# A replicated row in float32 and a carry copy taken out of the scan's signal, in a layer of scan attention and a gated expert network

## The chip, the cores and the metric

The kernel runs on all 8 cores of one Trainium2 chip. Each core takes one of the 8 sequences (2048 tokens of 1024 features); nothing passes between cores. The metric is the device time of the slowest core, in microseconds (us). Engines are named as the profile names them: PE is TensorE's matmul unit, PEld its weight load, DVE VectorE, ACT ScalarE, POOL GpSimd, SP SyncE.

## The reference

```
x = x + attn(layernorm(x));   x = x + ffn(layernorm(x))

attn(x):  h = rmsnorm(x) * gamma
          q, kv, a = split(h @ w_qkva.T)          # 3 x 1024
          y[t] = sigmoid(a[t]) * y[t-1] + kv[t]   # a scan over the 2048 tokens
          return q * y
ffn(x):   gate = softmax(x @ Wg + bg)             # 8 experts
          h = relu(x @ W1[e] + b1[e])             # 1024 -> 128, each expert
          return sum over e of gate[e] * (h @ W2[e] + b2[e])
```

## The kernel before

Everything is held transposed: features on the 128 partitions (8 blocks of 128, `KC = 8`), tokens along the free axis. The 2048 tokens are worked in 4 chunks of `TC = 512`. The whole program is written out by hand, engine by engine: each step is emitted with its engine, and counting semaphores (`s_mm` for PE, `s_dve`, `s_act`, `s_gp`) carry the waits. A semaphore counts the instructions of its engine, so "wait for the scan of block j" means "wait until DVE's count has reached the number that was recorded at that point" (`rec`, `rec_i`). What stands in an engine's queue is done in that order.

One chunk c goes through these steps.

- **Statistics 1** (`emitS1`, `emitSq`, `emitS2`): PE sums x and x squared over the features by a matmul with a column of 1/1024 (L288, L331). `emit_rows` (L218 to L235, DVE) makes one row of means and one of inverse variances, 512 long, on a single partition; ACT takes the square root of the latter (L242). DVE's reciprocal of one row is L235.
- **Replication 1** (`emitRep1`): two matmuls with a contraction of one row copy the two rows to all 128 partitions of PSUM (L347: 1/sigma, L349: mean); ACT takes both to SBUF in one activation (L357, `rm_bf`). DVE then subtracts and multiplies (L370, L384, in chunk 0 L873, L876).
- **emitB**: for each block j eight matmuls for kv (L415), eight for a (L434), two blocks later eight for q (L483). ACT takes the sigmoid (L446), DVE runs the scan (L457) and copies its last column to `carry` (L461), which the next chunk's scan starts from. kv of block j waits for the count recorded as `scan[j-2]`. DVE multiplies by q (L494), POOL adds x (L506).
- **emitC, emitRep2, emitLn2**: ACT casts the result (L521) and squares it (L543), PE sums (L533, L551), `emit_rows` and L242 again, then **replication 2** (L567: 1/sigma, L569: mean) into `ps_rep`. DVE copies both to SBUF for POOL (L577, L578) and normalizes blocks 0 to 4 (L589, L592); POOL does blocks 5 to 7 (L601, L604).
- **Gate and experts**: scores (L627), exp (L635), sum (L645), reciprocal (L656). The gate's reciprocal row is replicated to 8 partitions by a float32 matmul (L668, weights `ones_f`), read by DVE at L678. `emitE1`: eight matmuls for each expert (L724), relu on ACT (L784), the gate replicated (L742, L774), their product on DVE (L755, L805).
- **emitY2grp, emitOuts**: the second expert matmul (L826, L829) and the last addition (L843). For chunk c-1 these stand between the steps of chunk c.

The load of the next chunk's `xbf` is issued by POOL after its last addition of L506, and PE's statistics 1 of chunk c+1 stand in its queue ahead of replication 2 of chunk c. Replication 1 of chunk c+1 stands inside `emitE1` of chunk c, after the matmuls of expert 4. The weights' folds by gamma are L199 (DVE, chunk 0 only).

Of the kernel before, what the change touches and what calls it, by code (L numbers as in the profile page):

```python
# [27 lines left out]
def build_program(T=2048, TC=512):  # L28
# [23 lines left out]
    with stack:  # L52
# [24 lines left out]
        asig = sb("asig", [128, 2, TC], F32)  # L77
        h1g = sb("h1g", [128, E, TC], BF16)
        carry = sb("carry", [128, KC], F32)
        rows = sb("rows", [1, 5 * TC], F32)  # L80
        plscr = sb("plscr", [1, 1], F32)
        rows_bf = sb("rows_bf", [1, 2 * TC], BF16)
        exg = sb("exg", [8, TC], BF16)
        g_bf = sb("g_bf", [8, TC], BF16)

# [2 lines left out]

        def row(i):
            return rows[0:1, i * TC:(i + 1) * TC]  # L90
        R_M, R_T0, R_S2, R_INV, R_GI = 0, 1, 2, 3, 4

        def rowbf(i):
            return rows_bf[0:1, i * TC:(i + 1) * TC]
# [120 lines left out]
        def emit_rows(K, key, eps_add, key_m=None):  # L215
            def _rows(vector):
                vector.wait_ge(s_mm.h, K[key_m or key])
                s_dve.inc(vector.tensor_copy(row(R_M), ps_q[0:1, 0, :]))  # L218
                rec(K, key + "_rdm", s_dve)
                vector.wait_ge(s_dve.h, s_dve.n)  # L220
                s_dve.inc(vector.tensor_copy(rowbf(0), row(R_M)))
                s_dve.inc(vector.tensor_mul(row(R_T0), row(R_M), row(R_M)))
                vector.wait_ge(s_dve.h, s_dve.n)
                vector.wait_ge(s_mm.h, K[key])
                s_dve.inc(vector.scalar_tensor_tensor(row(R_S2), row(R_T0), -1.0,
                                                      ps_q[0:1, 1, :], ALU.mult,
                                                      ALU.add))
                rec(K, key + "_rd", s_dve)
                vector.wait_ge(s_dve.h, s_dve.n)
                if eps_add is None:  # L230
                    s_dve.inc(vector.tensor_scalar_max(row(R_S2), row(R_S2), 1e-33))
                else:
                    s_dve.inc(vector.tensor_scalar_add(row(R_S2), row(R_S2), eps_add))
                vector.wait_ge(s_dve.h, s_dve.n)
                ii = vector.reciprocal(row(R_INV), row(R_S2))  # L235
                s_dve.inc(ii)
            on("vector", _rows)
            rec(K, key + "_row1", s_dve)

            def _r(scalar):  # L240
                scalar.wait_ge(s_dve.h, K[key + "_row1"])
                ii = scalar.activation(rowbf(1), row(R_INV), AF.Sqrt)  # L242
                s_act.inc(ii)
            on("scalar", _r)
            rec(K, key + "_actr", s_act)

# [95 lines left out]
        def emitRep1(c):  # L342
            K = ck[c]

            def _rep(tensor):
                tensor.wait_ge(s_act.h, K["mm_s2_actr"])
                tensor.matmul(ps_q[:, 0, :], ones_bf[0:1, :], rowbf(1),  # L347
                              start=True, stop=True)
                ii = tensor.matmul(ps_q[:, 1, :], ones_bf[0:1, :], rowbf(0),  # L349
                                   start=True, stop=True)  # L350
                s_mm.inc(ii)
# [39 lines left out]
        def emitB(c):  # L391
# [9 lines left out]
            for j in range(KC):  # L401
# [52 lines left out]
                def _scan(vector, j=j):  # L454
# [2 lines left out]
                    s_dve.inc(vector.tensor_tensor_scan(y_sb[:, j, :], asig[:, j % 2, :],  # L457
                                                        ps_kv[:, j % 2, :], init,
                                                        ALU.mult, ALU.add))
                    vector.wait_ge(s_dve.h, s_dve.n)  # L460
                    ii = vector.tensor_copy(carry[:, j:j + 1], y_sb[:, j, TC - 1:TC])  # L461
                    s_dve.inc(ii)
                on("vector", _scan)
                rec_i(K["scan"], j, s_dve)

                if j >= 2:
                    emit_q(c, j - 2)
# [92 lines left out]
        def emitRep2(c):  # L560
            K = ck[c]

            def _rep(tensor):
                tensor.wait_ge(s_act.h, K["mm_s2b_actr"])
                if c > 0:
                    tensor.wait_ge(s_dve.h, ck[c - 1]["h1g"][E - 1])
                tensor.matmul(ps_rep[:, 0, :], ones_bf[0:1, :], rowbf(1),  # L567
                              start=True, stop=True)
                ii = tensor.matmul(ps_rep[:, 1, :], ones_bf[0:1, :], rowbf(0),  # L569
                                   start=True, stop=True)  # L570
# [436 lines left out]
```

## Time and profile before

| what | value |
|---|---|
| median of 2 runs | 511.88 us (511.72 to 512.03) |
| the profiled execution, its own time | 511.4 us |
| its span on core 0, the slowest | 509.9 us |
| spans of the 8 cores | 497.2 to 509.9 us |
| busy PE / DVE / ACT / POOL | 397.4 / 236.7 / 113.6 / 102.0 us |
| mean granted TensorE clock, core 0 | 0.894 of full speed |

The profile records one execution. A span runs from a core's first to its last instruction; 1.5 us of the execution's time lie outside it. "Busy" adds up the instructions' durations, so it tells how much an engine has to do and not whether the end waits for it. A matmul's duration holds its way through the array; the distance between the starts of two matmuls in a row tells what one costs in a stream.

### The profile page before, as it was taken

What the parts mean: (1) busy time and instruction counts of PE and PEld (TensorE: products, weight loads), DVE (VectorE), ACT (ScalarE), POOL (GpSimd) and SP (SyncE); (2) the same over time, 40 slices, a digit from 0 to 9 for tenths busy, and PEclk for the clock granted to TensorE, in tenths of its full rate; (3) what the DMA queues carried; (4) which work ended last, traced back from release to release, by engine and by line L of the source; (5) the groups of instructions that cost most, each with busy time, mean ns of one, the idle gap of its engine ahead of it and who ended that gap; (6) DMA issues with size and microseconds to landing.
All of it is one profiled execution on the core that took longest, in us unless ns stands there. A gap on an engine that the chain in (4) does not pass through costs nothing.

```text
span 509.9 us, 4752 instructions; the slowest of 8 cores (497.2 to 509.9 us)
## 1 busy us (share of the span) xinstructions
PE 397.4 (78%) x1532; PEld 146.3 (29%) x1532; DVE 236.7 (46%) x356; ACT 113.6 (22%) x179; POOL 102.0 (20%) x76
## 2 busy tenths in 40 slices
PE   1425399834778999759879999759989998888893
PEld 0101144300222444213323444213323443233331
DVE  0364433443466434337475344427475343783221
ACT  1220001350124112610222102610233115402200
POOL 6000012402800021308300023109100113050000
PEclk9955789986597999978988999978999999999997
DMA  7999995091000000560400000740400000004004
GB/s 137 214 171 156 160 171 86 0 227 21 0 0 2 0 1 1 144 104 1 165 1 1 1 0 2 170 77 1 165 0 2 1 0 1 1 0 165 2 0 165
DMA packets 18231, 32.06 MB, mean 63 GB/s; under 512 B 656, under 2 KB 4752, under 8 KB 18208
## 3 DMA queue, kind: packets, MB, share of 16 engines
q0 software_dynamic: 9584, 14.98, 19.5%
q1 hardware_dynamic: 8624, 16.79, 10.1%
q8 instruction: 13, 0.21, 0.2%
q14 instruction: 10, 0.08, 0.1%
HBM read 38.35 MB, written 8.39 MB: 92 GB/s over the span
## 4 chain that ended last, share of the span: by engine, by line
PE 60%; DMA 17%; DVE 11%; issue 3%; ACT 2%; another core or an unknown queue 2%; POOL 1%; DVEq 0%; ACTq 0%; POOLq 0%
PE ps_kv L415 11%; PE ps_a L434 10%; PE ps_q L483 10%; DMA xbf<-xT 10%; PE ps_kv L724 8%; DMA wq_bf<-wqT 8%; PE ps_a L829 6%; PE ps_kv L829 3%; DVE rows L235 3%; PE ps_a L724 3%; PE ps_q L288 2%; PE ps_a L627 1%; PE ps_rep L774 1%; DVE wq_bf L199 1%
## 5 line engine op out<-in xcount | busy, mean ns | idle before, releaser
L506 POOL TENSOR_TENSOR x_sb<-x_sb,y_sb 128x512 f32<-128x512 f32 x32 | 40.5, 1266 | 268.3 <-DVE y_sb L494 268.2
L415 PE MATMUL ps_kv<-hbf,wq_bf 128*128 128x512 bf16 x256 | 67.4, 393 | 18.0 <-DVE carry L461 8.3
L434 PE MATMUL ps_a<-hbf,wq_bf 128*128 128x512 bf16 x256 | 62.7, 389 | 4.9 <-DVE wq_bf L199 4.9
L457 DVE TENSOR_TENSOR_SCAN y_sb<-asig,carry,ps_kv 128x512 f32<-128x512 f32 x24 | 30.7, 1280 | 62.5 <-ACT asig L446 62.5
L483 PE MATMUL ps_q<-hbf,wq_bf 128*128 128x512 bf16 x256 | 59.2, 379 | 0.0
L446 ACT ACTIVATE asig<-ps_a 128x512 f32<-128x512 f32 x32 | 19.1, 597 | 158.8 <-PE ps_a L434 158.8
L724 PE MATMUL ps_kv<-hbf,w_bf 128*128 128x512 bf16 x192 | 48.6, 407 | 0.0
L288 PE MATMUL ps_q<-xbf,statc 128*1 128x512 bf16 x32 | 14.4, 624 | 36.5 <-DMA xbf<-xT 36.5
L415 PEld LDWEIGHTS ps_kv<-hbf,wq_bf 128*128 128x128 bf16 x256 | 25.3, 99 | 55.8 <-issue 30.4
L434 PEld LDWEIGHTS ps_a<-hbf,wq_bf 128*128 128x128 bf16 x256 | 25.3, 100 | 36.9 <-issue 8.7
L829 PE MATMUL ps_a<-h1g,w_bf 128*128 128x512 bf16 x128 | 34.0, 414 | 0.0
L483 PEld LDWEIGHTS ps_q<-hbf,wq_bf 128*128 128x128 bf16 x256 | 25.0, 98 | 30.2 <-issue 0.6
L829 PE MATMUL ps_kv<-h1g,w_bf 128*128 128x512 bf16 x128 | 31.9, 394 | 0.0
L601 POOL TENSOR_TENSOR y_sb<-x_sb,asig 128x512 f32<-128x512 f32 x12 | 15.2, 1267 | 79.6 <-DVE asig L578 79.6
L805 DVE TENSOR_TENSOR h1g<-y_sb,ps_rep 128x512 bf16<-128x512 f32 x24 | 16.2, 685 | 23.8 <-ACT y_sb L784 16.3
L235 DVE RECIPROCAL rows<-rows 1x512 f32<-1x512 f32 x8 | 26.7, 3341 | 0.8
L724 PEld LDWEIGHTS ps_kv<-hbf,w_bf 128*128 128x128 bf16 x192 | 18.7, 103 | 26.2 <-issue 9.0
L784 ACT ACTIVATE y_sb<-ps_kv,b1s 128x512 f32<-128x512 f32 x24 | 16.0, 677 | 43.2 <-PE ps_kv L724 43.2
L494 DVE TENSOR_TENSOR y_sb<-ps_q,y_sb 128x512 f32<-128x512 f32 x32 | 22.1, 691 | 7.4 <-PE ps_q L483 6.5
L218 DVE COPY rows<-ps_q 1x512 f32<-1x512 f32 x8 | 5.4, 676 | 34.5 <-PE ps_q L288 18.0
L315 POOL TENSOR_TENSOR tbf<-xbf 128x4096 bf16<-128x4096 bf16 x3 | 21.0, 7012 | 0.0
L211 ACT ACT_TABLE_LOAD x16 | 20.5, 1283 | 1.5 <-ACT y_sb L784 0.4
(82 smaller groups left out, 382.7 us busy)
## 6 DMA issues: line engine op xcount, KB each, us to landing
x_sb<-xT SPq DMA_DIRECT2D x4, 2048.0 KB, 13.2
outT<-x_sb SPq DMA_DIRECT2D x4, 2048.0 KB, 6.9
wq_bf<-wqT POOLq DMA_DIRECT2D x3, 2048.0 KB, 39.3
xbf<-xT POOLq DMA_DIRECT2D x3, 1024.0 KB, 16.3
w_bf<-w1p POOLq DMA_DIRECT2D x1, 2048.0 KB, 63.8
w_bf<-w2p POOLq DMA_DIRECT2D x1, 2048.0 KB, 75.6
xbf<-xT POOLq DMA_DIRECT2D x2, 512.0 KB, 11.9
wg_bf<-wgp POOLq DMA_DIRECT2D x1, 256.0 KB, 75.6
```

The lines of the kernel that those rows point to most:

```text
L211: ii = scalar.activation(plscr[:], plscr[:], func)
L235: ii = vector.reciprocal(row(R_INV), row(R_S2))
L288: ii = tensor.matmul(ps_q[0:1, 0, :], statc[:], xbf[:, k, :], start=(k == 0), stop=(k == KC - 1))
L315: ii = gpsimd.tensor_tensor(xsq[:], xbf[:], xbf[:], ALU.mult)
L415: ii = tensor.matmul(ps_kv[:, j % 2, :], wq_bf[:, k, (8 + j) * 128:(9 + j) * 128], hbf[:, k, :], start=(k == 0), stop=(k == KC - 1))
L434: ii = tensor.matmul(ps_a[:, j % 2, :], wq_bf[:, k, (16 + j) * 128:(17 + j) * 128], hbf[:, k, :], start=(k == 0), stop=(k == KC - 1))
L457: s_dve.inc(vector.tensor_tensor_scan(y_sb[:, j, :], asig[:, j % 2, :], ps_kv[:, j % 2, :], init, ALU.mult, ALU.add))
L483: ii = tensor.matmul(ps_q[:, j % 2, :], wq_bf[:, k, j * 128:(j + 1) * 128], hbf[:, k, :], start=(k == 0), stop=(k == KC - 1))
L494: ii = vector.tensor_tensor(y_sb[:, j, :], ps_q[:, j % 2, :], y_sb[:, j, :], ALU.mult)
L506: ii = gpsimd.tensor_tensor(x2buf(c)[:, j, :], x_sb[:, j, :], y_sb[:, j, :], ALU.add)
L724: ii = tensor.matmul(pb[:, BM[e] % 2, :], w1_bf[:, k, e * 128:(e + 1) * 128], hbf[:, k, :], start=(k == 0), stop=(k == KC - 1))
L829: ii = tensor.matmul(pb[:, d % 2, :], w2_bf[:, e, d * 128:(d + 1) * 128], h1g[:, e, :], start=False, stop=(e == E - 1))
```

## The change

Two things change. First, the row of 1/sigma is written by ACT in float32 (a new row `R_R` of `rows`, which grows from 5 to 6 rows; `rows_bf` shrinks to one) and not in bfloat16, and both matmuls that replicate it (L347, and L567 which becomes L569) take float32 weights (`ones_f`) and this float32 row. The row of means stays bfloat16. There are 8 such matmuls: replication 1 and replication 2 of 4 chunks. Second, the count that others wait for as `scan[j]` is recorded right behind the scan and no longer behind the carry copy, and in the last chunk, which no other follows, the copy and DVE's wait for the scan ahead of it are left out (8 copies of 32).

```diff
--- before.py
+++ after.py
@@ -77,9 +77,9 @@
         asig = sb("asig", [128, 2, TC], F32)
         h1g = sb("h1g", [128, E, TC], BF16)
         carry = sb("carry", [128, KC], F32)
-        rows = sb("rows", [1, 5 * TC], F32)
+        rows = sb("rows", [1, 6 * TC], F32)
         plscr = sb("plscr", [1, 1], F32)
-        rows_bf = sb("rows_bf", [1, 2 * TC], BF16)
+        rows_bf = sb("rows_bf", [1, TC], BF16)
         exg = sb("exg", [8, TC], BF16)
         g_bf = sb("g_bf", [8, TC], BF16)
 
@@ -88,7 +88,7 @@
 
         def row(i):
             return rows[0:1, i * TC:(i + 1) * TC]
-        R_M, R_T0, R_S2, R_INV, R_GI = 0, 1, 2, 3, 4
+        R_M, R_R, R_T0, R_S2, R_INV, R_GI = 0, 1, 2, 3, 4, 5
 
         def rowbf(i):
             return rows_bf[0:1, i * TC:(i + 1) * TC]
@@ -239,7 +239,7 @@
 
             def _r(scalar):
                 scalar.wait_ge(s_dve.h, K[key + "_row1"])
-                ii = scalar.activation(rowbf(1), row(R_INV), AF.Sqrt)
+                ii = scalar.activation(row(R_R), row(R_INV), AF.Sqrt)
                 s_act.inc(ii)
             on("scalar", _r)
             rec(K, key + "_actr", s_act)
@@ -344,7 +344,7 @@
 
             def _rep(tensor):
                 tensor.wait_ge(s_act.h, K["mm_s2_actr"])
-                tensor.matmul(ps_q[:, 0, :], ones_bf[0:1, :], rowbf(1),
+                tensor.matmul(ps_q[:, 0, :], ones_f[0:1, :], row(R_R),
                               start=True, stop=True)
                 ii = tensor.matmul(ps_q[:, 1, :], ones_bf[0:1, :], rowbf(0),
                                    start=True, stop=True)
@@ -457,11 +457,13 @@
                     s_dve.inc(vector.tensor_tensor_scan(y_sb[:, j, :], asig[:, j % 2, :],
                                                         ps_kv[:, j % 2, :], init,
                                                         ALU.mult, ALU.add))
-                    vector.wait_ge(s_dve.h, s_dve.n)
-                    ii = vector.tensor_copy(carry[:, j:j + 1], y_sb[:, j, TC - 1:TC])
-                    s_dve.inc(ii)
+                    rec_i(K["scan"], j, s_dve)
+                    if c + 1 < NCH:
+                        vector.wait_ge(s_dve.h, s_dve.n)
+                        ii = vector.tensor_copy(carry[:, j:j + 1],
+                                                y_sb[:, j, TC - 1:TC])
+                        s_dve.inc(ii)
                 on("vector", _scan)
-                rec_i(K["scan"], j, s_dve)
 
                 if j >= 2:
                     emit_q(c, j - 2)
@@ -564,7 +566,7 @@
                 tensor.wait_ge(s_act.h, K["mm_s2b_actr"])
                 if c > 0:
                     tensor.wait_ge(s_dve.h, ck[c - 1]["h1g"][E - 1])
-                tensor.matmul(ps_rep[:, 0, :], ones_bf[0:1, :], rowbf(1),
+                tensor.matmul(ps_rep[:, 0, :], ones_f[0:1, :], row(R_R),
                               start=True, stop=True)
                 ii = tensor.matmul(ps_rep[:, 1, :], ones_bf[0:1, :], rowbf(0),
                                    start=True, stop=True)
```

PE's queue in chunk 0, from the gate of expert 3 over replication 1 of chunk 1 to the matmuls of expert 5 (`g_bf` is the gate, `sel_bf` the selection matrix, `w_bf` the experts' weights). Before:

```order
L774 MATMUL ps_rep<-g_bf,sel_bf 128x512
L724 MATMUL ps_a<-hbf,w_bf 128x512 x8
L347 MATMUL ps_q<-rows_bf,ones_bf 128x512
L349 MATMUL ps_q<-rows_bf,ones_bf 128x512
L774 MATMUL ps_rep<-g_bf,sel_bf 128x512
L724 MATMUL ps_a<-hbf,w_bf 128x512 x8
```

and now:

```order
L776 MATMUL ps_rep<-g_bf,sel_bf 128x512
L726 MATMUL ps_a<-hbf,w_bf 128x512 x8
L347 MATMUL ps_q<-rows,ones_f 128x512
L349 MATMUL ps_q<-rows_bf,ones_bf 128x512
L776 MATMUL ps_rep<-g_bf,sel_bf 128x512
L726 MATMUL ps_a<-hbf,w_bf 128x512 x8
```

Nothing has moved; L347 alone reads `rows` and `ones_f`, both float32, in the place of `rows_bf` and `ones_bf`.

DVE's queue at the end of `emitB` in the last chunk: the last two scans (the order calls them SCALAR_TENSOR_TENSOR, the profile TENSOR_TENSOR_SCAN), the products with q and the start of the statistics. Before:

```order
L457 SCALAR_TENSOR_TENSOR y_sb<-asig,carry,ps_kv 128x512
L461 COPY carry<-y_sb 128x1
L494 TENSOR_TENSOR y_sb<-ps_q,y_sb 128x512
L457 SCALAR_TENSOR_TENSOR y_sb<-asig,carry,ps_kv 128x512
L461 COPY carry<-y_sb 128x1
L494 TENSOR_TENSOR y_sb<-ps_q,y_sb 128x512 x3
L218 COPY rows<-ps_q 1x512
```

and now:

```order
L457 SCALAR_TENSOR_TENSOR y_sb<-asig,carry,ps_kv 128x512
L496 TENSOR_TENSOR y_sb<-ps_q,y_sb 128x512
L457 SCALAR_TENSOR_TENSOR y_sb<-asig,carry,ps_kv 128x512
L496 TENSOR_TENSOR y_sb<-ps_q,y_sb 128x512 x3
L218 COPY rows<-ps_q 1x512
```

The copies are gone, so each product with q stands right behind a scan. In the chunks 0 to 2 they stand as before.

## Rows read from the trace of the kernel before

A row of the timeline gives the start (us from the span's start), the duration in us (of all, from the first start to the last end, where xN follows), the engine, the line, the operation, output<-input, and in brackets the idle time of the engine before it and what ended that.

**Rows 1.** The page's chain of work that ended last, shares of the span by engine.
```profile
PE 60%; DMA 17%; DVE 11%; issue 3%; ACT 2%; another core or an unknown queue 2%; POOL 1%; DVEq 0%; ACTq 0%; POOLq 0%
```

**Rows 2.** Timeline, chunk 0: first scan, its carry copy, and kv of block 2.
```profile
60.40 1.21 DVE L457 TENSOR_TENSOR_SCAN y_sb<-asig,ps_kv 128x512 f32<-128x512 f32 x1
61.72 0.15 DVE L461 COPY carry<-y_sb 128x1 f32<-128x1 f32 x1
...
62.02 3.57 PE L415 MATMUL ps_kv<-hbf,wq_bf 128*128 128x512 bf16 x8 [8.31 <-DVE carry L461]
```

**Rows 3.** Timeline, chunk 3: replication 2, then the float32 replication of the gate.
```profile
442.98 0.37 PE L567 MATMUL ps_rep<-rows_bf,ones_bf 1*128 1x512 bf16 x1 [1.43 <-ACT rows_bf L242]
...
443.67 0.69 DVE L577 COPY asig<-ps_rep 128x512 f32<-128x512 f32 x1 [0.53 <-PE ps_rep L569]
...
452.76 1.89 PE L627 MATMUL ps_a<-hbf,wg_bf 128*128 128x512 bf16 x8 [0.69 <-DVE x_sb L843]
...
465.35 1.02 PE L668 MATMUL ps_a<-rows,ones_f 1*8 1x512 f32 x2
...
466.54 0.68 DVE L678 TENSOR_TENSOR g_bf<-exg,ps_a 8x512 bf16<-8x512 bf16 x1 [5.51 <-PE ps_a L668]
```

**Rows 4.** Timeline, chunk 1: replication 2 and what follows until the scores.
```profile
228.69 0.60 PE L567 MATMUL ps_rep<-rows_bf,ones_bf 1*128 1x512 bf16 x1
...
229.82 0.69 DVE L577 COPY asig<-ps_rep 128x512 f32<-128x512 f32 x1 [8.50 <-PE ps_rep L569]
...
230.08 3.59 PE L829 MATMUL ps_a<-h1g,w_bf 128*128 128x512 bf16 x8
...
237.96 1.27 POOL L604 TENSOR_TENSOR hbf<-y_sb,asig 128x512 bf16<-128x512 f32 x1
...
240.19 1.89 PE L627 MATMUL ps_a<-hbf,wg_bf 128*128 128x512 bf16 x8
```

**Rows 5.** Timeline, chunk 0: replication 2 and the experts' first three groups.
```profile
121.19 0.56 PE L567 MATMUL ps_rep<-rows_bf,ones_bf 1*128 1x512 bf16 x1
...
122.07 0.69 DVE L577 COPY asig<-ps_rep 128x512 f32<-128x512 f32 x1 [9.15 <-PE ps_rep L569]
...
133.74 7.76 PE L724 MATMUL ps_kv<-hbf,w_bf 128*128 128x512 bf16 x24
```

**Rows 6.** Timeline, chunk 0: end of replication 1 for chunk 1, next matmul.
```profile
152.91 0.63 PE L349 MATMUL ps_q<-rows_bf,ones_bf 1*128 1x512 bf16 x1
...
154.32 0.58 PE L774 MATMUL ps_rep<-g_bf,sel_bf 8*128 8x512 bf16 x1 [0.78 <-DVE h1g L805]
```

**Rows 7.** Timeline, chunk 1: the same for chunk 2, and expert 5.
```profile
263.95 0.37 PE L347 MATMUL ps_q<-rows_bf,ones_bf 1*128 1x512 bf16 x1 [2.45 <-ACT rows_bf L242]
...
265.38 0.58 PE L774 MATMUL ps_rep<-g_bf,sel_bf 8*128 8x512 bf16 x1 [0.84 <-DVE h1g L805]
...
265.90 3.59 PE L724 MATMUL ps_a<-hbf,w_bf 128*128 128x512 bf16 x8
```

**Rows 8.** Timeline, chunk 2: expert 5 behind replication 1 for chunk 3.
```profile
378.65 1.90 PE L724 MATMUL ps_a<-hbf,w_bf 128*128 128x512 bf16 x8
```

**Rows 9.** Timeline, start: replication 1 of chunk 0 evacuated, then the fold.
```profile
29.75 1.00 ACT L357 ACTIVATE rm_bf<-ps_q 128x1024 bf16<-128x1024 f32 x1
...
31.08 3.26 DVE L199 TENSOR_SCALAR wq_bf<-wq_bf,gam 128x1024 bf16<-128x1024 bf16 x8 [3.53 <-DMA wq_bf<-wqT]
```

**Rows 10.** Groups by line and form: xcount, then busy us, mean ns, idle before.
```profile
L446 ACT ACTIVATE asig<-ps_a 128x512 f32<-128x512 f32 x32 | 19.1, 597 | 158.8 <-PE ps_a L434 158.8
...
L242 ACT ACTIVATE rows_bf<-rows 1x512 bf16<-1x512 f32 x8 | 5.0, 628 | 59.2 <-DVE rows L235 59.2
```

**Rows 11.** Timeline, last chunk: the product behind the last carry copy.
```profile
425.38 0.69 DVE L494 TENSOR_TENSOR y_sb<-ps_q,y_sb 128x512 f32<-128x512 f32 x1
```

**Rows 12.** Windows, PE: stretch, length, busy (matmuls), granted clock, DMA share, GB/s.
```profile
229.00:232.00 3.00, 3.00 (x8) 0.50 0.00 0
...
265.00:268.00 3.00, 2.62 (x6) 0.50 0.00 0
```

## The prediction

> **What bounds the kernel now.** I read the chain of waits first, then the waits in total, then the timeline around the eight replications. The chain lies on PE for 60% of the span, 17% on DMA, 11% on DVE [rows 1]. PE is not busy all the time, but nearly all that it waits for waits in turn for PE: the load of the next chunk is issued only after the last product of q, and the statistics rows are made from PE's sums. So a delay of PE at most places moves the end by as much, and what must be asked at each of the eight replications is whether PE or DVE stood waiting for something else there. The carry copies are 0.15 us each and DVE is busy for 236.7 of 509.9 us, so they matter only where somebody waits for the signal behind them.
>
> **One float32 replication.** The trace has this form once in each chunk, on the gate's row. One such matmul is recorded in two parts that take 1.02 us together, and DVE starts 1.19 us after its start (466.54 - 465.35) [rows 3]. A bfloat16 matmul at the same clock takes 0.37 us, and DVE starts 0.69 us after the first of the two of replication 2 (443.67 - 442.98) [rows 3]; one of them costs (1.90 - 0.37)/7 = 0.22 us in a stream [rows 8], so a single one would release DVE after 0.47 us. The float32 form thus costs 1.02 - 0.37 = 0.65 us more by durations and 1.19 - 0.47 = 0.72 us by release; I take 0.70. It is 0.65/0.22 = 3 further passes. At half clock a pass is (3.59 - 0.60)/7 = 0.43 us [rows 4], so the extra is 3 x 0.43 = 1.28 us there.
>
> The row of the trace loads 8 columns of weights and the new matmuls load 128; a load of bfloat16 weights of 128 columns shows no cost of its own: the distance of 0.22 us above holds one for each matmul. I take 0 and keep +0.2 us for each of the four on the path as the bound (one more pass is 0.22 us), 0.8 in all. The Trainium skill ("TensorE: Matmul & The Clock Gate", section on weight-path perf modes and on LDWEIGHTS) says that the fast weight load isn't used for float32 weights and that a plain load takes the columns divided by 1.2 GHz, 107 ns for 128. No row here shows a float32 load of that width. If two such loads were needed and none were hidden, the estimate by that page is some 0.2 us for each matmul, and the sum below would be 0.8 us higher.
>
> **Replication 2, four times.** In chunk 3 the clock is full. DVE waits for the second matmul (0.53 us, at 443.67) and then works without a pause until the scores, where PE stands 0.69 us waiting for DVE (452.76) [rows 3]. The whole delay goes through: +0.70.
> In chunk 1 (chunk 2 reads the same) the clock is at 0.50 [rows 12]: DVE starts 1.13 us after the first matmul (229.82 - 228.69) and PE goes on at once with L829, eight matmuls in 3.59 us [rows 4]. The extra is 1.28 us. Does DVE's delay show? POOL's last block is ready at 237.96 + 1.27 = 239.23, and its matmul is the last of eight that start at 240.19 [rows 4], about 2.5 us later; both move. So PE alone decides. The clock comes back within L829 in any case; where this moment stays, 1.28 us of matmuls at half speed are pushed out and done later in 0.64 us, and the net cost is 1.28 - 0.64 = +0.64. Where the clock comes back as much later, it is +1.28. I take 0.64 each, 1.3 for both, bounds 1.3 to 2.6.
> In chunk 0 the clock is between the levels: 0.56 us for the first matmul, DVE starts 0.88 us after it (122.07 - 121.19) [rows 5]. Here DVE's normalization paces PE until the scores, and PE idles between; the delay of 0.65 to 1.28 us goes through to 133.74. From there the experts' 24 matmuls take 7.76 us [rows 5], against about 24 x 0.22 = 5.3 us at full clock; half of the delay can be given back as above. I take +0.7, bounds 0.3 to 1.3.
> Sum: 0.7 + 1.3 + 0.7 = +2.7.
>
> **Replication 1, four times.** In chunk 0 ACT's evacuation ends at 30.75, while DVE is in the fold from 31.08 to 34.34 and reads its result only then [rows 9]. A delay of 1.28 us is hidden by 3.6 us of slack: 0. For chunk 2 the two matmuls start at 263.95 and free PE after 2 x 0.22 us, at 264.39, but PE waits for DVE's h1g until 265.38 [rows 7]: slack 0.99 us against 0.70, so 0; chunk 3 has the same shape: 0. This cover is DVE's wait for ACT's relu, which stands behind the square root and not behind the replication. If it were gone, each would cost 0.70. For chunk 1 the clock is at half: 152.91 + 0.43 = 153.34, the next matmul at 154.32 [rows 6]: slack 0.98 against 1.28, so +0.3. ACT's evacuation (L357) also comes later, and with it relu of expert 4, but PE needs that only behind expert 6. Sum: +0.3, bounds 0 to 0.6.
>
> **ACT's float32 row.** L242 takes 628 ns; a write of float32 by L446 takes 597 ns, from PSUM [rows 10]. On the path it is met seven times. I take 0, bounds 7 x 0.03 = 0.2 both ways.
>
> **The signal of the scan.** Only one wait of PE names the copy: kv of block 2 in chunk 0, 8.31 us, ended by the copy. The scan ends at 61.61, the copy at 61.87, PE starts 0.15 us later [rows 2]. With the signal behind the scan PE starts at 61.76: -0.26 us, of which half is lost if the clock, which is at half there too, comes back at the same moment. Behind it PE runs without a pause to the end of the chunk, so it reaches the end: -0.2. All other kv groups find their scan long done: 0. The longer row buffers move nothing in time: 0.
>
> **The last chunk's copies.** The last product of q that stands behind a copy starts at 425.38 [rows 11] and would start some 0.17 us earlier (the copy and a wait for it). The last q matmuls wait for it by at most 0.1 us, since PE has a group of its own until then. -0.1, bounds -0.17 to 0.
>
> **Sum.** 2.7 + 0.3 - 0.2 - 0.1 = +2.7 us. The profiled execution took 511.4 us (span 509.9, 1.5 outside), 0.5 less than the median; it becomes 514.1, and the median 511.9 + 2.7 = **514.6 us**, half a per cent slower. A measurement of this kernel tells about 2% (10 us) from no change for sure, so this counts as within 2%.
>
> **Rivals.**
> *The float32 work keeps the clock up.* Behind replication 1 for chunk 2 the clock is at 0.50 (265 to 268) [rows 12] and expert 5 takes 3.59 us [rows 7]; one chunk later it takes 1.90 [rows 8]. If 0.70 us more of matmul there were enough to stay at full clock, 1.69 us would come back for expert 5 and about half as much (0.85) for the next group, in chunk 1 and perhaps as much in chunk 0: 2.7 - 2 x 2.5 = -2.3, 509.6 us. The Trainium skill ("TensorE: Matmul & The Clock Gate", "What's actually happening") states the rule on which this rests: the throttled state is the default and activity releases it. Against it: PE had stood 2.45 us before the replication and 0.84 us behind it [rows 7]; 0.70 us more of work fills a fifth of that. Chance 0.08.
> *The clock comes back late and falls once more.* This is the slower side. The start of PE's work relative to the moment at which the clock changes is shifted by 0.3 to 1.3 us. If after each of the three loads one more group of eight runs at half clock (3.59 for 1.90: 3 x 1.69 = 5.1) and chunk 2's replication 1 is followed by a fall as in chunk 1 (1.69 + 0.85 = 2.5), the sum is 2.7 + 5.1 + 2.5 = +10.3, 522.2 us, just over 2%. It needs all four; each alone is 1.7 to 2.5 us. Chance of all 0.03; of one or two (516 to 519 us), 0.12.
> *The change costs nothing.* If PE takes these one-row float32 matmuls in a single pass, or the slack at the four replications 2 is larger than read, only the scan's -0.3 is left: 511.6 us. Against it: the same form, also of one row, takes 1.02 us in four chunks. Chance 0.07.
> *The loads move.* DMA holds 17% of the chain [rows 1]; the eight cores load at nearly the same time, and their order may shift. 17% of 509.9 us is 87 us; the three loads of `xbf` and the start share it. If each of the three lands 1 us sooner or later, it is 3 us: 511.6 or 517.6. Chance 0.1, both ways alike.
> *The forecast*, 513.5 to 516 us: 0.6.
>
> **Numbers.** The bounds of the terms add to 511.88 + (0.7 + 1.3 + 0.3 + 0 - 0.2 - 0.26 - 0.17) = 513.6 below and 511.88 + (0.7 + 2.6 + 1.3 + 0.6 + 0.2 + 0.8) = 518.1 above. Below stand three of the rivals; I go to 510.5 and to 518.5. Faster by over 2%: 0.01; within 2%: 0.95; slower: 0.04.
>
> **What would show it.** The profile after should have L347 and L569 (the former L567) in two parts of float32, 1.0 us at full clock; DVE's start behind replication 2 at 1.4 us (chunk 3) in place of 0.69; PE's wait ahead of L774's successor shorter but not gone; kv of block 2 in chunk 0 named as waiting for the scan. I am wrong if the two stages between replication 2 and the scores take no longer, if the float32 weights cost visibly more than 0.1 us each, or if the clock's low stretches lengthen or vanish.

## The result, and the profile after

The changed kernel takes 516.97 us (median of 11 runs, 515.51 to 520.08) against 512.38 us for the kernel before (10 runs, 511.72 to 514.07). The ratio is 1.0092, with a 95% interval of 1.0067 to 1.0118: 4.6 us more, 0.9%, which lies within 2% and is still outside the measurement's own scatter. The forecast was 514.6 us, +2.7. In some executions of any of these kernels a part of the cores reads a lower granted clock than the others and the time is some per cent longer; the ratios here and below leave such executions out.

The profiled execution took 516.22 us. The view by core shows spans of 504.6 to 514.7 us; the lowest granted clock stands beside the longest span.

```profile
core 4: 505.2 us, clock 0.897
core 5: 514.7 us, clock 0.872
```

In the chain that ended last PE has gained 2 points against [rows 1], and it is busy for 410.0 us where it was busy for 397.4 (each the slowest core of its execution); the other engines are where they were. The mean granted clock of the eight cores went from 0.900 to 0.887. None of this names a cause, so the reading has to go to the stages.

```profile
PE 410.0 (80%) x1540; PEld 149.9 (29%) x1540; DVE 234.9 (46%) x348; ACT 114.0 (22%) x179; POOL 102.0 (20%) x76
...
PE 62%; DMA 17%; DVE 11%; issue 3%; ACT 2%; another core or an unknown queue 2%; POOL 1%; DVEq 0%; ACTq 0%; POOLq 0%
```

**The scan's signal.** The timeline of core 5 in chunk 0, which answers to [rows 2]:

```profile
61.42 1.21 DVE L457 TENSOR_TENSOR_SCAN y_sb<-asig,ps_kv 128x512 f32<-128x512 f32 x1
62.74 0.15 DVE L463 COPY carry<-y_sb 128x1 f32<-128x1 f32 x1
...
62.78 3.33 PE L415 MATMUL ps_kv<-hbf,wq_bf 128*128 128x512 bf16 x8 [7.42 <-DVE y_sb L457]
```

The wait now names the scan, and PE starts 1.36 us after the scan's start (62.78 - 61.42) in place of 1.62 (62.02 - 60.40 in [rows 2]): the 0.26 us that the prediction read, to the hundredth.

**Replication 2 of chunk 3**, answering to [rows 3], on two cores of the same execution, core 5 first and core 1 second:

```profile
445.53 1.09 PE L569 MATMUL ps_rep<-rows,ones_f 1*128 1x512 f32 x2 [1.42 <-ACT rows L242]
...
446.94 0.69 DVE L579 COPY asig<-ps_rep 128x512 f32<-128x512 f32 x1 [1.25 <-PE ps_rep L571]
...
446.98 2.62 PE L831 MATMUL ps_a<-h1g,w_bf 128*128 128x512 bf16 x8
...
450.07 2.55 PE L831 MATMUL ps_a<-h1g,w_bf 128*128 128x512 bf16 x8
...
456.76 1.89 PE L629 MATMUL ps_a<-hbf,wg_bf 128*128 128x512 bf16 x8
```

```profile
446.76 1.09 PE L569 MATMUL ps_rep<-rows,ones_f 1*128 1x512 f32 x2 [1.43 <-ACT rows L242]
...
448.22 1.90 PE L831 MATMUL ps_a<-h1g,w_bf 128*128 128x512 bf16 x8
...
457.26 1.89 PE L629 MATMUL ps_a<-hbf,wg_bf 128*128 128x512 bf16 x8 [0.69 <-DVE x_sb L845]
```

DVE starts 1.41 us after the first matmul (446.94 - 445.53) where it was 0.69: +0.72. Core 1 reaches the scores after 10.50 us (457.26 - 446.76); before it was 9.78 (452.76 - 442.98 in [rows 3]). Core 5 needs 11.23 us (456.76 - 445.53): its two groups L831 take 2.62 and 2.55 us where core 1 has 1.90, and PE no longer waits for DVE ahead of the scores. The view by windows shows why, core 5 and then core 1 (columns: stretch, length, busy with the count of matmuls, granted clock, DMA share, GB/s):

```profile
444.00:447.00 3.00, 1.58 (x6) 1.00 0.02 5
447.00:451.00 4.00, 4.00 (x13) 0.63 0.00 0
```

```profile
448.00:451.00 3.00, 3.00 (x14) 1.00 0.00 0
```

On core 5 the granted clock falls to its lower level (1.2 GHz) just behind the replication, and comes back. Ahead of the fall PE had stood 1.42 us, worked on one-row matmuls for some 1.4 us and begun on its normal load. Six of the eight cores show this fall in the changed kernel; in the kernel before, none does.

**Replication 2 at half clock.** Chunk 0 and chunk 1 of core 5, answering to [rows 5] and [rows 4]:

```profile
121.86 2.07 PE L569 MATMUL ps_rep<-rows,ones_f 1*128 1x512 f32 x2
...
123.72 0.63 PE L571 MATMUL ps_rep<-rows_bf,ones_bf 1*128 1x512 bf16 x1
...
124.46 0.69 DVE L579 COPY asig<-ps_rep 128x512 f32<-128x512 f32 x1 [11.76 <-PE ps_rep L571]
...
231.44 2.07 PE L569 MATMUL ps_rep<-rows,ones_f 1*128 1x512 f32 x2
...
234.30 3.59 PE L831 MATMUL ps_a<-h1g,w_bf 128*128 128x512 bf16 x8
...
238.36 2.59 PE L831 MATMUL ps_a<-h1g,w_bf 128*128 128x512 bf16 x8
```

DVE starts 2.60 us after the first matmul (124.46 - 121.86); with bfloat16 at half clock it was 1.13 [rows 4]. The extra is 1.47 us, not 1.28. In chunk 1 a whole group runs at half clock and the next one still in part (2.59 us); in the kernel before, core 0 had 3.59 us for the first [rows 4] and 1.92 for the next.

**The weights.** The view of one line by operation (count, then min/median/max in ns), with the gate's eight-column form last:

```profile
L347 PEld LDWEIGHTS ps_q<-rows,ones_f x8: 181/281/328, 27.7 to 376.7; 1*128 1x128 f32 x8
```

```profile
L349 PEld LDWEIGHTS ps_q<-rows_bf,ones_bf x4: 93/146/146, 28.7 to 377.6; 1*128 1x128 bf16 x4
```

```profile
L670 PEld LDWEIGHTS ps_a<-rows,ones_f x8: 80/82/83, 143.7 to 469.4; 1*8 1x8 f32 x8
```

Eight loads for four matmuls: one for each of the two recorded parts. A float32 load of 128 columns takes 181 ns at full clock and up to 328 at half, a bfloat16 one 93 and 146.

**Stage by stage.** From the timelines of all eight cores I took the starts of PE's named lines and averaged the distances. In chunks 1 to 3 the stages from kv to the sum over the result (L533, 43.57 us) and from the scores to the gate's reciprocal (12.59) are the same in both kernels within 0.1 us, on every core; these are not:

| stage, mean of 8 cores, us | before | after | difference | predicted |
|---|---|---|---|---|
| chunk 0, replication 2 to scores | 3.76 | 4.76 | +1.00 | +0.7 |
| chunk 1, the same | 10.69 | 12.37 | +1.68 | +0.64 |
| chunk 2, the same | 10.40 | 11.17 | +0.77 | +0.64 |
| chunk 3, the same | 9.84 | 11.05 | +1.21 | +0.70 |
| replication 1 to kv, for chunk 1 | 11.22 | 11.15 | -0.07 | +0.3 |
| the same, for chunk 2 | 11.71 | 11.45 | -0.26 | 0 |
| the same, for chunk 3 | 10.59 | 11.60 | +1.01 | 0 |
| gate's reciprocal of chunk 3 (L668) to the last group of L829 | 33.74 | 35.00 | +1.26 | 0 |
| q to replication 2, loads and all the rest | | | -1.9 | -0.3 |
| sum, first replication 1 to the last group of L829 | 466.9 | 471.6 | +4.7 | +2.7 |

Behind each later replication 1 PE waited for DVE before its next matmul (L774), 0.63 to 1.20 us on every core of the kernel before. In the changed kernel 0.09 to 0.49 us of this wait are left on some cores and nothing on the others: in chunk 2 on six of eight, in chunk 3 on seven.

### The profile page after: what moved, and what is told of

The parts are those of the page before. It is cut to its first block, busy times and chain, and to the rows that moved or that the text cites. A ratio compares the mean times of both kernels' runs of the same rounds, so it can differ in the third digit from the quotient of the medians.

```text
span 514.7 us, 4752 instructions; the slowest of 8 cores (504.6 to 514.7 us)
## 1 busy us (share of the span) xinstructions
PE 410.0 (80%) x1540; PEld 149.9 (29%) x1540; DVE 234.9 (46%) x348; ACT 114.0 (22%) x179; POOL 102.0 (20%) x76
## 4 chain that ended last, share of the span: by engine, by line
PE 62%; DMA 17%; DVE 11%; issue 3%; ACT 2%; another core or an unknown queue 2%; POOL 1%; DVEq 0%; ACTq 0%; POOLq 0%
PE ps_kv L415 11%; PE ps_q L485 10%; PE ps_a L434 10%; DMA xbf<-xT 9%; PE ps_kv L726 8%; DMA wq_bf<-wqT 8%; PE ps_a L831 6%; PE ps_kv L831 3%; PE ps_a L726 3%; DVE rows L235 3%; PE ps_q L288 2%; PE ps_a L629 1%; PE ps_rep L776 1%; DVE wq_bf L199 1%
## 5 line engine op out<-in xcount | busy, mean ns | idle before, releaser
L288 PE MATMUL ps_q<-xbf,statc 128*1 128x512 bf16 x32 | 14.4, 622 | 35.0 <-DMA xbf<-xT 35.0
L831 PE MATMUL ps_a<-h1g,w_bf 128*128 128x512 bf16 x128 | 34.2, 415 | 0.0
L831 PE MATMUL ps_kv<-h1g,w_bf 128*128 128x512 bf16 x128 | 31.8, 393 | 0.0
L726 PEld LDWEIGHTS ps_kv<-hbf,w_bf 128*128 128x128 bf16 x192 | 18.6, 102 | 25.8 <-issue 8.2
## 6 DMA issues: line engine op xcount, KB each, us to landing
x_sb<-xT SPq DMA_DIRECT2D x4, 2048.0 KB, 13.8
xbf<-xT POOLq DMA_DIRECT2D x2, 512.0 KB, 11.9
```

The costliest lines, as they stand in the source:

```text
L288: ii = tensor.matmul(ps_q[0:1, 0, :], statc[:], xbf[:, k, :], start=(k == 0), stop=(k == KC - 1))
L726: ii = tensor.matmul(pb[:, BM[e] % 2, :], w1_bf[:, k, e * 128:(e + 1) * 128], hbf[:, k, :], start=(k == 0), stop=(k == KC - 1))
L831: ii = tensor.matmul(pb[:, d % 2, :], w2_bf[:, e, d * 128:(d + 1) * 128], h1g[:, e, :], start=False, stop=(e == E - 1))
```

## The experiments

A ratio is that to the kernel before in the same set of runs, with its 95% interval; one hundredth is 5.1 us. Sets ran at different times and on two chips, so ratios are compared, not times.

**1. One part alone.** Two kernels that divide the change. The first has the float32 replications, and not the scan's signal and the last chunk's copies:

```diff
-                ii = scalar.activation(rowbf(1), row(R_INV), AF.Sqrt)
+                ii = scalar.activation(row(R_R), row(R_INV), AF.Sqrt)
...
-                tensor.matmul(ps_q[:, 0, :], ones_bf[0:1, :], rowbf(1),
+                tensor.matmul(ps_q[:, 0, :], ones_f[0:1, :], row(R_R),
...
-                tensor.matmul(ps_rep[:, 0, :], ones_bf[0:1, :], rowbf(1),
+                tensor.matmul(ps_rep[:, 0, :], ones_f[0:1, :], row(R_R),
```

> The change without its carry part: the 8 float32 replications alone, carry copies and scan signal as before. Theory 'passes' (the cost is the longer matmul itself): the four replications 2 cost about 0.7 us each at full clock and up to 1.5 at half, so +3 to +3.5 us over before, and the whole change is 0.3 us less than this. Theory 'clock' (the float32 form also moves or adds low stretches of the clock): +4.5 to +5.5 us, mean granted clock lower than before by about 0.01, and again within 0.5 us of the whole change.

Measured: 515.6 us, ratio 1.0064 (1.0043 to 1.0086), +3.3 us. In chunk 3 four of eight cores fall and take 11.24 us, the others 10.51.

The second has bfloat16 replications and the other part:

```diff
+                    rec_i(K["scan"], j, s_dve)
+                    if c + 1 < NCH:
-                    vector.wait_ge(s_dve.h, s_dve.n)
-                    ii = vector.tensor_copy(carry[:, j:j + 1], y_sb[:, j, TC - 1:TC])
+                        vector.wait_ge(s_dve.h, s_dve.n)
+                        ii = vector.tensor_copy(carry[:, j:j + 1],
+                                                y_sb[:, j, TC - 1:TC])
...
-                rec_i(K["scan"], j, s_dve)
```

> The carry part alone, bfloat16 replications. Both theories: -0.2 to -0.3 us, not told from no change. If it came out slower by more than 1 us, the carry part would have moved the phase of the work against the clock, and the float32 matmuls would be cleared of that share.

Measured: 511.46 us, ratio 0.9988 (0.9976 to 1.0001), -0.6 us. Chunk 3's stage takes 9.78 to 9.87 on the eight cores. So the float32 part is the cost; the other part is not told from nothing, and agrees with the predicted -0.3. It also shows that the +1.01 us ahead of chunk 3's kv isn't the float32's alone: this stage reads 11.77 us here, without any float32. It has a few fixed values: 8.85 us (three cores of the kernel before), 11.5 to 11.9, and 10.5 on one core of the changed kernel.

**2. Which replication.** Float32 in replication 2 alone (ACT writes the float32 row for `mm_s2b` and the bfloat16 one otherwise), and in replication 1 alone:

```diff
-                ii = scalar.activation(rowbf(1), row(R_INV), AF.Sqrt)
+                dst = row(R_R) if key == "mm_s2b" else rowbf(1)
+                ii = scalar.activation(dst, row(R_INV), AF.Sqrt)
```

> Float32 only in the four replications 2 (replication 1 stays bfloat16, no carry part). 'Passes': nearly all of e1, +3 us, since replication 1 hides in PE's wait for DVE. 'Clock': +3 to +4.5, with the fall of the clock behind replication 2 of the last chunk on most cores (from its start to the scores 11.2 us in place of 9.8).

> Float32 only in the four replications 1. 'Passes': 0 to +0.5 us, hidden but for chunk 1 at half clock. 'Clock': +1 to +2, the stretch from replication 1 to kv of the next chunk longer in the last of the three (8.9 us on some cores before, 11.7 after).

Measured: replication 2 alone 514.01 us, ratio 1.0047 (1.0033 to 1.0062), +2.4 us; replication 1 alone 512.33, ratio 1.0016 (1.0003 to 1.0029), +0.8 us. The two add up to the 3.3 us of experiment 1. In replication 1's kernel chunk 3's stage stays at 9.79 us. So replication 2 carries three quarters and replication 1 little, as predicted, by these midpoints. In this execution with float32 in replication 2 no core falls in chunk 3, and its mean stage there is 10.54: the fall is no fixed part of the price.

**3. Float32, or three more passes of anything?** The kernel before, with the 1/sigma replication issued four times in bfloat16 (three results are overwritten):

```diff
-                tensor.matmul(ps_rep[:, 0, :], ones_bf[0:1, :], rowbf(1),
-                              start=True, stop=True)
+                for _ in range(4):
+                    tensor.matmul(ps_rep[:, 0, :], ones_bf[0:1, :], rowbf(1),
+                                  start=True, stop=True)
```

The same for replication 1.

> The kernel before with each replication of 1/sigma issued four times in bfloat16 into the same bank, in place of once: about the PE time of the float32 form (4 x 0.22 = 0.87 us at full clock, 4 x 0.43 = 1.7 at half) in ordinary matmuls; no float32 row, no carry part. 'Passes': the same as the float32 part alone, +3 us (ratio 1.006). 'Clock' (the float32 form counts for less than its time when the clock is set): fewer low stretches than there, +1.5 to +2.5 us, and from replication 2 of the last chunk to the scores 10.5 us on every core, never the 11.2 that float32 shows on about half of them.

Measured: 519.7 us against 514.23 in its set, ratio 1.0094 (1.0058 to 1.013). The timeline of core 1:

```profile
445.92 1.02 PE L569 MATMUL ps_rep<-rows_bf,ones_bf 1*128 1x512 bf16 x4 [1.43 <-ACT rows_bf L242]
...
447.31 2.50 PE L831 MATMUL ps_a<-h1g,w_bf 128*128 128x512 bf16 x8
```

Four bfloat16 passes take 1.02 us, like one float32 matmul with eight columns of weights [rows 3], and the group behind them takes 2.50 us: the clock falls here too, on four of eight cores. So the float32 format isn't needed for the fall; more one-row work behind PE's wait does it as well.

This run also splits the length. At full clock DVE starts 1.34 us after the first matmul (447.26 - 445.92), which is 0.65 more than the 0.69 of [rows 3], where float32 has 0.72 more. At half clock, chunk 1 of the same core:

```profile
231.08 1.88 PE L569 MATMUL ps_rep<-rows_bf,ones_bf 1*128 1x512 bf16 x4
...
233.50 0.69 DVE L579 COPY asig<-ps_rep 128x512 f32<-128x512 f32 x1 [9.24 <-PE ps_rep L571]
```

That is 2.42 us where one pass gives 1.13 [rows 4]: +1.29, the predicted 1.28, where float32 has +1.47. Three passes are thus priced rightly at both levels, and what float32 adds beyond them is 0.07 us at full clock and 0.18 at half.

**4. Does PE's wait ahead of it matter?** The changed kernel with six full matmuls in front of chunk 3's replication 2, in the time in which PE waits for ACT (their result is overwritten):

```diff
-                tensor.wait_ge(s_act.h, K["mm_s2b_actr"])
...
+                if c == NCH - 1:
+                    for _ in range(6):
+                        tensor.matmul(ps_rep[:, 0, :], w2_bf[:, 0, 0:128],
+                                      w2_bf[:, 0, 0:512], start=True, stop=True)
+                tensor.wait_ge(s_act.h, K["mm_s2b_actr"])
                 tensor.matmul(ps_rep[:, 0, :], ones_f[0:1, :], row(R_R),
```

> The changed kernel with six matmuls into ps_rep, whose result is overwritten, put ahead of replication 2 of the last chunk, where PE waits 1.4 us for ACT's row. 'Passes': they fill a wait, no change against the changed kernel (+4.5 over before). 'Clock': the fall behind this replication goes away, 10.5 us from it to the scores on all cores, and the time is 0.5 to 1.5 us less than the changed kernel's (ratio to before 1.006 to 1.008).

The timeline of core 0:

```profile
448.71 1.46 PE L570 MATMUL ps_rep<-w_bf 128*128 128x512 bf16 x6
...
450.19 1.09 PE L573 MATMUL ps_rep<-rows,ones_f 1*128 1x512 f32 x2
...
451.64 1.90 PE L835 MATMUL ps_a<-h1g,w_bf 128*128 128x512 bf16 x8
```

The fall is gone on all eight cores, and the stage is 10.51 us on each. The whole kernel isn't faster, against the 1.006 to 1.008 that was expected of it: 520.45 us, ratio 1.0122 (1.0075 to 1.0169). The stage gives back 0.5 us in the mean, which this interval can't show; the total says nothing for or against it. One execution without a fall proves little by itself, since experiment 2 has one without any filler; experiment 7 repeats it.

**5. Away from the wait for the load.** PE's queue is in order, and L288 of the next chunk stands ahead of replication 2 and waits for its data. Moved behind the softmax sum, in bfloat16 (with the scan's part) and in the changed kernel:

```diff
                 if c + 1 < NCH:
                     emitLoadXbf(c + 1)
-                    emitS1(c + 1)
                 emitRep2(c)
...
                 emitSum(c)
+                if c + 1 < NCH:
+                    emitS1(c + 1)
                 emitSumInv(c)
```

> Bfloat16 replications and the carry part, and the statistics-1 sum of the next chunk (L288) moved on PE from ahead of replication 2 to behind the softmax sum. PE then does not wait for the next chunk's load ahead of replication 2: its wait of 9.5, 5.5 and 5.9 us should go, less what DVE needs in chunk 0. I expect -15 us (-10 to -19) against before, 497 us.

> The changed kernel (float32 replications, carry part) with the same move of L288. Replication 2 then starts at about full clock and behind a wait for ACT in all four chunks. 'Passes': it stays behind e7 by 4 x 0.7 = 2.9 us. 'Clock': the difference changes with the place of the low stretches, anything from 2 to 6 us.

Measured: 495.61 us in bfloat16 (4 runs, 495.27 to 495.88), ratio 0.9631 (0.9584 to 0.9678), and 501.1 with float32, ratio 0.9722 (0.9664 to 0.978). Both beat both kernels of this study. The waits in total say what went, first core 0 of the kernel before, then core 4 of the moved one in bfloat16 (us in total, times, longest):

```profile
PE ps_q L288 <- DMA xbf<-xT: 36.5, 5, 10.5
```

```profile
PE ps_q L288 <- DMA xbf<-xT: 17.0, 2, 11.4
```

Only the start's waits are left. The three waits of later chunks went, 19.5 us on these cores. The profiled executions' slowest cores differ by 15.7 us (509.9 and 494.2), the medians of the set by 18.6, and in this set the kernel before is itself some 2 us slower than in the others; I had expected 15. The pair is also a cleaner measurement of one replication 2, since nothing ahead of it waits for a load any more. Chunk 0 of core 4, bfloat16 first, then float32:

```profile
115.75 0.58 PE L569 MATMUL ps_rep<-rows_bf,ones_bf 1*128 1x512 bf16 x1 [5.61 <-ACT rows_bf L242]
...
116.86 0.69 DVE L579 COPY asig<-ps_rep 128x512 f32<-128x512 f32 x1 [1.98 <-PE ps_rep L571]
```

```profile
117.10 2.04 PE L569 MATMUL ps_rep<-rows,ones_f 1*128 1x512 f32 x2 [5.61 <-ACT rows L242]
...
119.67 0.69 DVE L579 COPY asig<-ps_rep 128x512 f32<-128x512 f32 x1 [3.44 <-PE ps_rep L571]
```

1.11 us against 2.57: +1.46 at half clock, and the stage takes 5.40 us for 3.93 on every core. In chunks 1 and 2 the clock is full on every core, and the stage takes 10.50 for 9.79, +0.71. These are the two sizes of one float32 replication 2, with no other effect in them.

In whole, float32 costs 0.9722 - 0.9631 = 0.0091 here too, 4.7 us, where 'passes' said 2.9. The four replications 2 make up 3.7 of it in the mean. Replication 1 isn't hidden: from it to kv of chunk 2 it is 11.82 us for 10.45 in the mean of eight cores, because PE's wait of 0.84 us behind it is used up and the groups behind it run longer at half clock.

And the pair has a fall behind the short form. In chunk 3 of the bfloat16 kernel core 4 alone takes 10.52 us where the other seven take 9.86 or 9.87:

```profile
425.74 0.37 PE L569 MATMUL ps_rep<-rows_bf,ones_bf 1*128 1x512 bf16 x1 [1.42 <-ACT rows_bf L242]
...
426.48 2.44 PE L831 MATMUL ps_a<-h1g,w_bf 128*128 128x512 bf16 x8
```

The granted clock of that core is 1.00 from 423 to 427 us and 0.62 from 427 to 430. With float32 two of eight fall. Counted over all profiled executions without fillers ahead of it, the clock falls behind chunk 3's replication 2 on 1 core of 32 with one bfloat16 pass there and on 19 of 48 with float32 or four passes. The longer work makes the fall likely; it is neither needed nor enough.

**6. The changed kernel again**, in the set of experiment 7.

> The changed kernel itself, unaltered, so that the fillers below are compared on one chip. +4.6 us over before (ratio 1.009, 1.007 to 1.012), and again some cores with 10.5 and some with 11.2 us from replication 2 of the last chunk to the scores.

Measured: 517.07 us, ratio 1.0107 (1.0089 to 1.0125). The result repeats, and the cost is 5.5 us in this set. Three of eight cores fall in chunk 3. The parts of experiment 1 add up to 0.52%, well below both measurements of the whole.

**7. Length and clock apart.** Both kernels with fillers: nine full matmuls ahead of replication 1 of each later chunk, six ahead of the last replication 2 (all overwritten). The edit is the same in both; here in the changed kernel:

```diff
+                if c > 0:
+                    tensor.wait_ge(s_dve.h, K["mm_s2_rd"])
+                    for _ in range(9):
+                        tensor.matmul(ps_q[:, 0, :], wq_bf[:, 0, 0:128],
+                                      wq_bf[:, 0, 0:512], start=True, stop=True)
                 tensor.wait_ge(s_act.h, K["mm_s2_actr"])
...
-                tensor.wait_ge(s_act.h, K["mm_s2b_actr"])
...
+                for _ in range(6 if c == NCH - 1 else 0):
+                    tensor.matmul(ps_rep[:, 0, :], wq_bf[:, 0, 0:128],
+                                  wq_bf[:, 0, 0:512], start=True, stop=True)
+                tensor.wait_ge(s_act.h, K["mm_s2b_actr"])
```

> The changed kernel with matmuls whose result is overwritten put into PE's waits for ACT's row: nine (1.9 us) ahead of each replication 1 of chunks 1 to 3, six (1.3 us) ahead of replication 2 of the last chunk. If the delay alone makes the change slower, nothing comes back (+4.6). If part of it is clock that falls around the replications, the stretch from replication 1 to kv shortens from 11.6 to 9 or 9.5 us, no core shows 11.2 us in the last chunk, and the kernel is 3 to 6 us faster than the changed one, about level with before.

> The kernel before with the same fillers. If the clock falls behind replication 1 in both kernels, this gains 3 to 6 us over before too, and the float32 cost that is left between this and the changed kernel with fillers is the matmuls' own length, some 3 us.

Measured, in one set with experiment 6: changed with fillers 509.93 us, ratio 0.9959 (0.9939 to 0.9979); before with fillers 506.15, ratio 0.9886 (0.9866 to 0.9906). The timeline of the changed kernel with fillers, core 3, ahead of replication 1 for chunk 2:

```profile
262.13 2.10 PE L349 MATMUL ps_q<-wq_bf 128*128 128x512 bf16 x9
...
264.17 1.12 PE L352 MATMUL ps_q<-rows,ones_f 1*128 1x512 f32 x2
...
265.65 1.90 PE L734 MATMUL ps_a<-hbf,w_bf 128*128 128x512 bf16 x8
```

Expert 5 takes 1.90 us where it took 3.59 [rows 7], and the stage from replication 1 to kv of chunk 2 shrinks from 11.7 to 8.8 us in the kernel before and from 11.5 to 9.0 in the changed one. No core of either kernel falls in chunk 3; the changed one takes 10.51 us there, the other 9.79. With fillers the change costs 0.9959 - 0.9886 = 0.0073, 3.7 us; without them 5.5. If so, some 3.7 us are length, and the rest, about 1.8 us, went with the clock. But each of the two differences is uncertain by about 1.5 us, so 1.8 isn't told from nothing by the times; that the clock has a share rests on the stages. The fillers themselves are worth 0.0114 (5.8 us) in the kernel before and 0.0148 (7.6 us) in the changed one.

**8. Late L288 and fillers together.** Experiment 5's bfloat16 kernel with the same fillers, six ahead of every later replication 2 and 24 in chunk 0.

> e7 (bfloat16, carry part, L288 late) with fillers: nine ahead of replication 1, six ahead of replication 2 in chunks 1 to 3, 24 ahead of that in chunk 0, where PE waits 5.6 us. Chunk 0 from replication 2 to the scores 3.5 in place of 3.9, L288 behind it 1.9 in place of 3.6 us at best; replication 1 to kv 8.9 in place of 10.4 to 12. In all -4 to -6 us against e7: 490 us, ratio 0.955 to before.

Measured: six executions with a median of 500.27 us and a lowest one of 487.05. In the profiled one cores 2 to 5 end after 481.9 to 485.2 us, the others after 496.8 to 498.5, and from 200 to 210 us core 0 reads a granted clock of 0.81 where core 2 reads 1.00. With 17.7 us between the lowest and the highest (504.72) there is no interval, and whether the two gains add stays open.

## Why the prediction was right in kind and too small in size

**The forecast** was +2.7 us, the result +4.6; it lies inside the range given (510.5 to 518.5) and above the forecast's own 513.5 to 516. By its own signs the prediction was wrong in two points, worked out below: the clock's low stretches did lengthen, and at half clock the float32 form costs more than 0.1 us beyond its passes.

**One replication at full clock, +0.70: right.** Measured 0.72 (DVE's start), 0.71 (experiment 5), 0.72 (chunk 3's stage on core 1). Three further passes, as worked out from the gate's row.

**At half clock, +1.28: too small.** Measured 1.47 and 1.46. The three passes were priced rightly (experiment 3: +1.29 for three bfloat16 passes more); the term that failed is the one for float32 weights of 128 columns, taken at 0. It shows between the two recorded parts. The second part of the gate's row, with eight columns, starts 0.43 us behind the first, two passes; with 128 columns it is 0.50 us at full clock, and at half 0.98 to 1.02 where two passes take 0.85. By DVE's start the float32 form costs 0.07 us beyond its passes at full clock (0.72 against experiment 3's 0.65) and 0.18 to 0.19 at half (1.47 against 1.29 or 1.28); the bound of 0.2 us each held, and at half clock it is nearly met. That it goes with the width of the weights is read from the gate's row at full clock; no run varies the width alone, and no gate's row at half clock stands beside it.

The Trainium skill ("TensorE: Matmul & The Clock Gate", on weight-path perf modes and LDWEIGHTS) says that float32 weights don't take the fast load, and the trace agrees: 181 ns for 128 columns of float32 beside 93 of bfloat16. The plain load itself is recorded as 181 ns at full clock and not as the 107 that the Trainium skill gives there. The estimate of 0.2 us for each matmul, worked out in the prediction from that figure, fits at half clock (0.19) and is too much at full (0.07).

**Replication 2 reaches the end: right.** All four stages grow, in the changed kernel and in experiment 5, and replication 2 carries most of the cost (experiment 2); there is no cover for it.

**The clock behind replication 2: this step failed.** The prediction let the clock of the kernel before stand. Its sentence "where this moment stays" set chunks 1 and 2 at +0.64 each, and its "the whole delay goes through" set chunk 3 at its bare length. In the profiled execution the four stages cost +4.66 us together where it had 2.7, chunk 1 +1.68 and chunk 3 +1.21. In chunk 3 the length is 0.72 and the other half is the fall of the clock on six of eight cores, which costs 0.73 us more where it happens (11.23 against 10.50). I had treated chunk 3 as safe, since the clock there was full before. Experiment 3 shows that one-row work lengthened by three passes brings the fall in either format (once, in experiment 5, it came behind the short form too), and with full matmuls in PE's wait no core of 16 has it (experiments 4 and 7). That the same holds of chunk 1 wasn't isolated: its stage varies from 10.5 to 13.8 us over the cores. Over the profiled executions that keep L288 in its place, its mean is 10.3 to 11.1 us in four bfloat16 ones and 11.2 to 12.9 in six with float32 in replication 2, so some +1.3 us is typical and the 1.68 of one execution is partly chance.

**Replication 1 costs +0.3: the size about right, the cover not.** Its kernel alone costs 0.8 us (0.15 to 1.5), and the stage for chunk 2 takes no longer in the changed kernel. But the slack of 0.99 us was set against a replication at full clock. There 0.1 us of PE's wait is left; where the clock is at half or falls, which the prediction reckoned with in chunk 1 alone, the wait is used up, and in experiment 5 that stage takes 1.37 us more. That chunk 3's stage lost its fast variant has another origin, as experiment 1's second kernel shows, and stays open.

**The scan's signal and the copies, -0.3: not refuted.** -0.26 is read directly for the signal; in whole it is -0.6 (-1.2 to +0.05), which doesn't exclude zero.

**The tail, taken at 0: wrong by 1.26 us in this execution.** From the gate's reciprocal of chunk 3 to the last group of L829 every profiled core of every run takes one of four times, about 31.3, 32.9, 34.5 or 35.7 us. Neither format owns one of them, but the fall does: in the five executions with float32 or four passes in replication 2 in which L288 keeps its place and no filler is added, all 17 cores that fall in chunk 3 show 35.7, and the 23 that don't show 32.9 or 34.5. So a fall in chunk 3 goes with 1.2 to 2.8 us more in the tail, beside its own 0.73. That is a count and no experiment: four cores with fillers show 35.8 or 35.9 without a fall, and the two that fall in experiment 5's float32 kernel show 31.3. The other way, PE that comes later waits less for the loads: from the sum over the result to replication 2 it is 1.6 us less over chunks 0 to 2, most of the -1.9. The two nearly cancel, and that the total stayed in the range is in part luck.

**The rivals.** "The clock comes back late and falls once more", in its part form (516 to 519 us, chance 0.12), is where the time came out. Of its places, one more group partly at half clock behind a load is seen in chunk 1 (2.59 us on core 5); the other, chunk 3 behind replication 2, it did not name. "Float32 keeps the clock up" is refuted for this kernel: with more work on PE the mean granted clock is lower, 0.887 for 0.900. "Costs nothing" falls with experiments 1 and 2. "The loads move" played a part of a microsecond or two, in favour of the change.

**What stays open.** Experiment 1's halves add up to 0.5% and the whole measures 0.9 to 1.1%, with intervals that don't meet for the second measurement. A phase between clock and work that only the two together hit would do it; so would the other chip. Why one core falls and another with the same instructions does not, and what ties the tail to the fall, isn't shown either. No run settles it.

## What to carry to other kernels

In this kernel a one-row float32 matmul in place of a bfloat16 one costs three further passes, and all of it shows wherever another engine stands waiting for its result; look first at who waits, since the four replications 1 cost 0.8 us alone and the four replications 2 2.4. A cover that is read at full clock has to be read at half clock too: 0.84 us of wait hides 0.70, not 1.28. When an edit lengthens thin work behind a stall of PE, price the clock as well: a fall on the next groups costs as much as the passes themselves, and full-clock rows of the kernel before don't promise full clock after. And read what stands at the head of an in-order queue before tuning a format: moving one group that waited for a load gave -3.7%, where the whole change of format costs 0.9%.

## What the chip showed that I had not expected

Discarded matmuls of full size, put into waits of PE, made both kernels faster: 0.0114 and 0.0148 of the time, 5.8 and 7.6 us, because the groups behind run in 1.90 in place of 3.59 us. A float32 replication costs 0.71 us at full clock and 1.46 at half, 0.07 and 0.18 us beyond three bfloat16 passes. And a fall of the clock is decided core by core: in one execution six cores take 11.24 us for a stage and two 10.51, with the same instructions.
